# Decoder layer on one core: decay exponents from broadcast running sums instead of TensorE

## What is computed

```python
xBCzA = einsum('bld,od->blo', u, W_in)           # u: layernorm of x
xBC   = causal_depthwise_conv(xBC, conv_w, conv_b)  # 4 taps
dt    = softplus(A_log)
cum   = cumsum(-dt, axis=2)                       # within chunks of 128 tokens
CB    = einsum('bcqhn,bckhn->bchqk', C, B)
diff  = cumT[..., :, None] - cumT[..., None, :]
decay = exp(where(tril, diff, -inf))
y_intra = einsum('bchqk,bckhp->bcqhp', CB * decay, xdt)
# and across chunks: state from B * exp(cum_last - cum), y_inter from C * exp(cum)
out   = einsum('bli,oi->blo', (y_intra + y_inter + D * x) * silu(z + z_bias), W_out)
```

## Time and profile before

| what | before |
|---|---|
| median of 3 runs | 405.5 us (405.41 to 407.51) |
| the profiled execution's own time | 406.83 us |
| its span | 405.1 us |
| granted TensorE clock, mean | 0.996 |
| PE busy | 386.7 us (95%) |
| VectorE (DVE) busy | 332.6 us (82%) |
| ScalarE (ACT) busy | 226.6 us (56%) |
| GpSimd (POOL) busy | 176.2 us (43%) |
| chain that ended last | PE 70%, DVE 13%, ACT 8%, issue 6%, POOL 2% |
| DMA moved | 21.13 MB |

### The profile page before, as it was taken

The page is one execution under the profiler, slowest core; times in us unless marked ns, Lnnn a source line. Parts: engine busy times, 40 slices in busy tenths (PEclk is TensorE's granted clock), DMA queues, the critical chain, the costliest instruction groups (busy, mean ns, idle before and its releaser), DMA issues.

```text
span 405.1 us, 8904 instructions
## 1 busy us (share of the span) xinstructions
PE 386.7 (95%) x3023; PEld 299.3 (74%) x3023; DVE 332.6 (82%) x564; ACT 226.6 (56%) x422; POOL 176.2 (43%) x208
## 2 busy tenths in 40 slices
PE   8998999999999999996989999899999999999996
PEld 8686676766766767764767777568888888888886
DVE  5988899999999999997989938738958759696685
ACT  6766556465565564568676632664554545546541
...
GB/s 186 100 54 25 58 64 8 115 56 61 62 59 28 41 59 63 61 35 109 128 49 25 49 162 1 0 2 1 60 19 78 3 78 13 65 0 2 0 2 104
DMA packets 35932, 21.13 MB, mean 52 GB/s; under 512 B 17048, under 2 KB 33760, under 8 KB 35904
## 3 DMA queue, kind: packets, MB, share of 16 engines
...
...
## 4 chain that ended last, share of the span: by engine, by line
PE 70%; DVE 13%; ACT 8%; issue 6%; POOL 2%; ACTq 0%; DVEq 0%; POOLq 0%
PE bank L1283 22%; PE bank L1259 10%; PE bank L1249 9%; PE bank L1478 8%; PE bank L1252 5%; PE bank L1398 3%; PE bank L1269 2%; PE bank L1466 2%; DVE conv L1228 2%; PE bank L1307 2%; PE bank L1425 2%; DVE conv L1021 2%; POOL el L656 1%; ACT conv L695 1%; PE bank L1486 1%
## 5 line engine op out<-in xcount | busy, mean ns | idle before, releaser
L1021 DVE SCALAR_TENSOR_TENSOR conv<-bank,taps,conv 128x510 f32<-128x510 f32 (+2 forms) x204 | 149.8, 745 | 17.4 <-ACT conv L695 12.3
L1283 PE MATMUL bank<-uth,parts 128*128 128x512 f32 x272 | 95.3, 407 | 1.1 <-DVE utl L1004 0.9
L695 ACT ACTIVATE conv<-bank,tap_b,taps 128x512 f32<-128x512 f32 x68 | 52.9, 777 | 69.6 <-PE bank L1283 58.9
L569 POOL TENSOR_TENSOR ce<-conv,ecx 128x512 f32<-128x512 f32 x15 | 19.4, 1291 | 117.5 <-DVE conv L1021 117.5
L1283 PEld LDWEIGHTS bank<-uth,parts 128*128 128x128 f32 x272 | 51.0, 187 | 18.9 <-issue 3.5
L651 POOL TENSOR_TENSOR ul<-conv,uh 128x512 fp32r<-128x512 f32 x32 | 42.9, 1357 | 40.5 <-ACT uh L922 27.5
L656 POOL TENSOR_TENSOR el<-conv,parts 128x512 fp32r<-128x512 f32 x30 | 44.3, 1504 | 30.3 <-ACT parts L934 30.3
L1283 PE MATMUL bank<-utl,parts 128*128 128x512 f32 x136 | 53.5, 393 | 0.0
L1216 DVE CAST uh<-conv 128x512 fp32r<-128x512 f32 x28 | 26.0, 966 | 22.5 <-ACT conv L918 21.9
L1228 DVE TENSOR_TENSOR conv<-conv 128x512 f32<-128x512 f32 x32 | 31.4, 1014 | 11.9 <-ACT conv L939 11.8
L1106 DVE SCALAR_TENSOR_TENSOR g<-dec,bank 128x512 f32<-128x512 f32 x64 | 40.8, 678 | 0.0
(11 more groups left out here) (208 smaller groups left out, 743.3 us busy)
## 6 DMA issues: line engine op xcount, KB each, us to landing
w_raw<-in_L_attn_W_in_dram SPq DMA_DIRECT2D x17, 256.0 KB, 3.2
ecx<-ecum_dram SPq DMA_DIRECT2D x32, 128.0 KB, 2.9
ew_raw<-in_L_ffn_Wup_dram SPq DMA_DIRECT2D x7, 256.0 KB, 2.9
ew_raw<-in_L_ffn_Wgate_dram SPq DMA_DIRECT2D x7, 256.0 KB, 3.1
ew_raw<-in_L_ffn_Wdown_dram SPq DMA_DIRECT2D x7, 256.0 KB, 3.8
...
out_dram<-xres SPq DMA_DIRECT2D x4, 256.0 KB, 2.1
...
```

What stands on the lines that cost most here:

```text
L695: act.activation(conv[q][:, j, HALF * h:HALF * (h + 1)], bank[u % 2][:], ACT.Identity, bias=tap_b[q][:, j:j + 1], scale=taps[q][:, j, TAPS ...
L1021: dve.scalar_tensor_tensor(out=dst[:, :, d:SEQ], in0=src[:, :, 0:SEQ - d], scalar=taps[q][:, j, TAPS - 1 - d:TAPS - d], in1=dst[:, :, d:SE ...
L1283: ins = pe.matmul(bank[u % 2][:], w, x_t, start=(i == 0), stop=(i == 3 * KD - 1))
```

## The change

The running sums cum go to DRAM as float32 and come back broadcast over all 128 partitions, 256 KB for each unit of a pair (`load_cumb`, two DMAs for each half), into four buffers `cumb`, one for each unit. GpSimd masks each with an affine_select (`mask`). For half 0 it adds the column -cum_s (`spans`), and ScalarE takes one exponential over 512 columns (`decays`). For half 1 ScalarE adds the column as the bias of its exponential, which takes four instructions of 128 columns for each unit (`decays_beside`). The column comes from PE (two transposes of cum at the start), is negated by ScalarE into `ncum`, and is copied for each pair by GpSimd (`copy_ncum`). The exponent matmuls, their tables and the bf16 parts are gone. `turn_w` moves into the place of the first exponents.

DVE's taps are crossed: of two quarters v and v+1 the order is (v,1), (v,2), (v+1,1), (v,3), (v+1,2), (v+1,3), and those of quarter 3 move from the start of body n to the end of body n-1. The work for the later stages moves to earlier bodies: the gates of z to 8 and 9, the pairwise terms to 10 and 11, gate_y(0) to 11 and 12, the weight splits to 13 and 14.

```diff
-    cum_dram = nc.dram_tensor("cum_dram", (3, NH * T, P), BF16, kind="Internal").ap()
+    cum_dram = nc.dram_tensor("cum_dram", (NH * T, P), F32, kind="Internal").ap()
...
-            def load_cum(m, q):
-
-                at_least(sp, expo_done, 4 * (m - 2))
...
+            def load_cumb(m, h):
+
+                at_least(sp, exp_done, 4 * (m - 2) + 2 * h + 2)
+                for j in range(2):
+                    row = T * (2 * (m - 1) + j) + T // 2 * h
+                    sp.dma_start(cumb[2 * h + j][:],
+                                 cum_dram[row:row + T // 2, :].partition_broadcast(P)).then_inc(cumb_in[h], 16)
...
-                if n == 1:
-                    sp.wait_ge(cr0_done, 1)
-                if n < PAIRS:
-                    load_cum(n + 1, 1 - q)
+                if n > 1:
+                    load_cumb(n, 1)
...
                     load_w(n + 3, 1 - q)
                 if n + 2 <= PAIRS:
                     load_taps(n + 2, q)
+                if n < PAIRS:
+                    load_cumb(n + 1, 0)
...
+            def copy_ncum(m, q):
+
+                src = ncum[:].rearrange("p c (b h) -> p h b c", b=NSEQ)
+                pool.tensor_copy(ncp[q][:], src[:, bass.ds(2 * (m - 1), 2), :, :]).then_inc(ncp_done, 1)
+
+            def mask(u):
+
+                pool.affine_select(out=cumb[u][:], in_=cumb[u][:], compare_op=ALU.is_ge, fill=NEG, base=0,
+                                   pattern=[[0, T // 2], [1, P]], channel_multiplier=-1).then_inc(masked, 1)
+
+            def spans(n, q, u):
+
+                pool.wait_ge(masked, 4 * (n - 1) + u + 1)
+                from_s = ncp[q][:, u, 0:2, :].rearrange("p b c -> p (b c)").unsqueeze(2).to_broadcast([P, T // 2, P])
+                pool.tensor_tensor(cumb[u][:], cumb[u][:], from_s, ALU.add).then_inc(span_done, 1)
...
+                pool.wait_ge(cumb_in[0], 32 * n)
+                pool.wait_ge(ncp_done, n)
                 if end:
+                    pool.wait_ge(cumb_in[1], 32 * n)
+                    for u in range(4):
+                        mask(u)
+                    spans(n, q, 0)
+                    spans(n, q, 1)
                     decay_c_half(n, q, 0)
                     decay_c_half(n, q, 1)
...
+                    gate_late()
+                    rest_weights(1, 1, 1)
+                    rest_weights(1, 1, 2)
+                    return
+                at_least(pool, stT_done, n - 1)
+                copy_xs(n + 1, 1 - q)
+                mask(0)
+                mask(1)
+                spans(n, q, 0)
+                spans(n, q, 1)
+                at_least(pool, y_done, 4 * (n - 1))
+                copy_x(n + 1, 1 - q)
+                decay_c(n, k, q)
+                pool.wait_ge(cumb_in[1], 32 * n)
+                at_least(pool, exp_done, 4 * (n - 1))
+                copy_ncum(n + 1, 1 - q)
+                mask(2)
+                mask(3)
+                if not isinstance(n, int):
+                    return
+                if n == 1:
+                    weigh_context()
+                if n in (PAIRS - 7, PAIRS - 6):
+
+                    for v in range(2 * (n - PAIRS + 7), 2 * (n - PAIRS + 7) + 2):
                         pool.wait_ge(zgate_done, v + 1)
                         pool.tensor_tensor(z_part(v), z_part(v), zgate(v), ALU.mult).then_inc(z_gated, 1)
...
+                if n in (PAIRS - 5, PAIRS - 4):
+                    pool.wait_ge(z_gated, 4)
+                    gate_y(0, n - PAIRS + 5)
+                if n == PAIRS - 3:
+                    pool.wait_ge(sig_done, T)
+                    pool.tensor_scalar(sig[:], sig[:], P_SEM / 2, P_SEM / 2, ALU.mult, ALU.add).then_inc(sig_scaled, 1)
+                    rest_weights(0, 0, 0)
+                if n == PAIRS - 2:
+                    rest_weights(0, 0, 1)
+                    rest_weights(0, 0, 2)
+                    rest_weights(1, 1, 0)
+                if n == PAIRS - 1:
+                    gate_y(1, 0)
+                    gate_y(1, 1)
...
             def decays(n, u):
-                a, b = 4 * (n - 1) + u, u % 2
-                act.wait_ge(expo_done, a + 1)
-                at_least(act, g_done, a - 1)
-                act.activation(dec[b][:], bank[4 + b][:], ACT.Exp).then_inc(exp_done, 1)
+                a = 4 * (n - 1) + u
+                act.wait_ge(span_done, 2 * (n - 1) + u + 1)
+                at_least(act, g_done, a - 3)
+                act.activation(dec[u][:], cumb[u][:].rearrange("p i t -> p (i t)"), ACT.Exp).then_inc(exp_done, 1)
+
+            def decays_beside(n, q, u, chunks):
+
+                if chunks[0] == 0:
+                    act.wait_ge(masked, 4 * (n - 1) + u + 1)
+                    act.wait_ge(ncp_done, n)
+                    at_least(act, g_done, 4 * (n - 2) + u + 1)
+                for i in chunks:
+                    ins = act.activation(dec[u][:, i * P:(i + 1) * P], cumb[u][:, i, :], ACT.Exp,
+                                         bias=ncp[q][:, u % 2, 2 + i // 2, i % 2:i % 2 + 1])
+                if chunks[-1] == T // 2 - 1:
+                    ins.then_inc(exp_done, 1)
...
+                decays_beside(n, q, 2, range(4))
                 if first:
                     act.wait_ge(y_init, 1)
                 else:
                     act.wait_ge(cb_done, 2 * (n - 1))
-                    act.wait_ge(ce_done, n - 1)
                 beside(n, m, km, r, 0)
+                decays_beside(n, q, 3, range(2))
                 beside(n, m, km, r, 1)
                 copy_b(n)
-                decays(n, 2)
-                decays(n, 3)
+                decays_beside(n, q, 3, range(2, 4))
                 copy_state_turned(n)
+                if not first:
+                    act.wait_ge(ce_done, n - 1)
                 beside(n, m, km, r, 2)
                 beside(n, m, km, r, 3)
...
+            def crossed_taps(m, q, v):
+
+                done = 12 * m + 3 * v
+                for i, (u, d) in enumerate(((v, 1), (v, 2), (v + 1, 1), (v, 3), (v + 1, 2), (v + 1, 3))):
+                    j, h = u // 2, u % 2
+                    src = bank[u % 2][:].rearrange("p (b l) -> p b l", b=2)
+                    dst = conv[q][:, j, HALF * h:HALF * (h + 1)].rearrange("p (b l) -> p b l", b=2)
+                    if d == 1:
+                        dve.wait_ge(acc_first, 4 * m + u + 1)
+                    else:
+                        dve.wait_ge(tap_done, done + (0, 1, 0, 2, 3, 5)[i])
+                    dve.scalar_tensor_tensor(
+                        out=dst[:, :, d:SEQ], in0=src[:, :, 0:SEQ - d], scalar=taps[q][:, j, TAPS - 1 - d:TAPS - d],
+                        in1=dst[:, :, d:SEQ], op0=ALU.mult, op1=ALU.add).then_inc(tap_done, 1)
...
-                        other_taps(n + 1, 1 - q, 0)
-                        other_taps(n + 1, 1 - q, 1)
+                        crossed_taps(n + 1, 1 - q, 0)
                     dve.wait_ge(exp_done, a + 1)
                     dve.wait_ge(cb_done, 2 * (n - 1) + u // 2 + 1)
                     at_least(dve, y_done, a - 1)
 
-                    dve.scalar_tensor_tensor(out=g[b][:], in0=dec[b][:], scalar=1.0, in1=bank[2 + b][:],
+                    dve.scalar_tensor_tensor(out=g[b][:], in0=dec[u][:], scalar=1.0, in1=bank[2 + b][:],
                                              op0=ALU.min, op1=ALU.mult).then_inc(g_done, 1)
                     if u == 3 and not last(n, 1):
-                        other_taps(n + 1, 1 - q, 2)
+                        crossed_taps(n + 1, 1 - q, 2)
...
-            pe.transpose(bank[7][:, 0:P], sdecT[:], ident[:]).then_inc(sdec_turned, 1)
+            pe.transpose(bank[7][:, 0:P], sdecT[:], ident[:])
+            for c in range(2):
+                ins = pe.transpose(bank[7][:, (1 + c) * P:(2 + c) * P], cum[:, c * P:(c + 1) * P], ident[:])
+            ins.then_inc(sdec_turned, 1)
...
-            def exponents(n, k, q, u):
-
...
-                for a in range(2):
-                    ins = pe.matmul(bank[4 + j][NS * a:NS * (a + 1), :], cl[q][:, j, NS * a:NS * (a + 1)],
-                                    cr[q][a][:, j, 4 * h:4 * h + 4, :].rearrange("p t k -> p (t k)"), start=True, stop=True)
-                ins.then_inc(expo_done, 1)
...
-                    exponents(n, k, q, 0)
-                    exponents(n, k, q, 1)
+                    turn_w(n + 2, k + 1, q, lambda: None)
                 else:
                     end_pair(n, k, q)
-                if not last(n, 2):
-                    turn_w(n + 2, k + 1, q, lambda: None)
                 b_dot_c(n, q, 0)
                 passes(m, r, 0, range(6))
                 passes(m, r, 1, range(6))
                 turn_b(n, q)
-                exponents(n, k, q, 2)
-                exponents(n, k, q, 3)
...
                 weigh(n - 1, 1 - q, 2)
-                exponents(n, k, q, 0)
-                exponents(n, k, q, 1)
+                if not last(n, 2):
+                    turn_w(n + 2, k + 1, q, lambda: None)
                 from_state(n - 1, 0)
```

186 lines of the change are left out of this document (57 added, 129 removed).

## The result

Slower: **461.1 us** (median of 4 runs, 457.2 to 462.2) against 405.8 before on the same chip, a ratio of 1.134 with a 95% interval of 1.126 to 1.141. The sign and the mechanism are as forecast; the 442 us are 19 us short, and the time is 2 us outside the range of 428 to 459. The profiled execution has a span of 459.0 us.

The account below looks back on a forecast made before the run. A loop through the SP queue was to set each pair at 14.8 us; start +3.2, pairs +22.3 and +0.5, tail +13.9, end -3.2 summed to +36.7 us, a median of 442.2, range 428 to 459.

Parts of the forecast that it names:

- The loop that is closed: Pair stage: half-0 loads queue behind the write of y, so each pair's y hangs on the last: 14.8 us per pair.
- Two loads: lands 3.2 us after its issue: In the pair's loop: the second half-0 load starts 0.65 us after the first and lands 3.2 us after issue.
- My own upper end, 3.8: Half-0 loads in the pair's loop: a landing of 3.8 us would make the loop 15.4 us.
- SP from Y(n-1) ... 6.04: In the pair's loop: SP's queue takes 6.04 us from ScalarE's copy of y to where the next half-0 load can start.
- GpSimd and ScalarE, 4.9: End of the pair's loop: GpSimd's copy, masks and additions 4.0 us, then ScalarE's second decay 0.5 and y copy 0.37.
- the line through 0.30 and 0.40: GpSimd's masks: affine_select times for 128 and 256 columns, extended to 0.60 us for 512.
- The clock: Rival: PE stands still for 3.5 of 14.8 us per pair, so its clock falls: 458 us, chance 0.08.
- The broadcast lands late: Rival in the pair's loop: dear masks or a landing of 4.6 us add 1.4 per pair: 462 us, chance 0.06.
- Tail: From ScalarE's copy of pair 13's y to pair 15's: 38.2 us against 24.3 today, +13.9.
- Start: Up to ScalarE's copy of pair 1's y: decay 1 ends later than today, +3.2 us.
- After Y(15): Behind ScalarE's copy of pair 15's y: PE has C·B, turn_b and the first output tile done, no exponents: -3.2 us.
- The queue does not bind: 397: Rival in the pair stage: SP's queue does not bind and pairs fall to DVE's 11.6 us: some 397, chance 0.05.

Follow-up runs that it names:

- the fillers: Eight extra 512-column matmuls per pair, from 1 to 15, placed where TensorE waits, added to the changed kernel: 454.8 us.
- the run with the four pieces: On top of the fillers, the write of the 1024 sums cut into four and the experts' loads put a pair later, behind half 0: 462.5 us.
- contiguous sums: On top of the fillers, the 1024 sums written to DRAM as 128 pieces of 32 bytes in place of 1024 of 4 bytes: 453.8 us.
- the queue open: Changed kernel with SyncE's part reordered, next pair's half-0 broadcast first and its half-1 broadcast last, late z and y loads spread over six parts: 433.9 us.

## Why the prediction was right, and where it failed

- **The loop that is closed**: right. Two more issues in the loop and moving the half-0 load both changed the pair as it says, and the plain pair at 14.78 us is the 14.8 forecast.
- **"Two loads: lands 3.2 us after its issue"**: this is the step that failed most, +11.0 us. The forecast has 0.65 + 3.2 = 3.85 from the first issue to GpSimd's start. It was 4.2 to 4.7 in plain pairs and 5.0 to 5.9 in the last four, 4.77 on average. The second issue came 0.47 behind the first. The first load landed 3.5 us after its issue in the median of the twelve pairs, near w_raw's 3.3, but the second, for which GpSimd waits as well, 4.2 on average (3.5 to 5.4). I had costed the second of two broadcasts as a lone load of weights. My own upper end, 3.8, was nearer. The three loads of experts' weights that stand behind half 0 at Y(9) and Y(10) are a part of it: issue to start is 5.5 and 5.2 there in after, 5.15 and 5.3 with the fillers. In the run with the four pieces they stood behind half 0 at Y(10) and Y(11) instead, and Y(9) fell to 4.6, Y(10) stayed at 5.2 and Y(11) rose from 4.1 to 5.1. In after the ones at Y(11) and Y(12) were 5.0 and 5.9 without such loads, and 4.1 and 4.6 with the fillers, for no reason that a run isolates. Nor did any run load a half without broadcast, so what a broadcast costs more than a plain load is not shown. The 2.6 us estimated from the Trainium skill (DMA: Bandwidth & Descriptors, section Anatomy of one DMA), which I had put aside, would have been further off.
- **"SP from Y(n-1) ... 6.04"**: right in the pairs without anything odd and 1.0 to 2.0 longer in four, +5.6 in all. One, +2.0 at Y(2), stands behind the write of the sums and was gone with contiguous sums. All four stand in pairs in which the instruction queue moved 16 KB during the issues (at 72.0 in the one at Y(2)); that was not tested, and how much of each it makes stays open.
- **GpSimd and ScalarE, 4.9**: 4.5 to 4.6 but for the pair at Y(7), as one addition takes 1.04 us and not the 1.29 of the product of C (1042 ns is the mean of one in the page's costliest groups). The masks were 0.61 to 0.64, as taken from the line through 0.30 and 0.40.

```profile
L498 POOL TENSOR_TENSOR cumb<-cumb,ncp 128x512 f32<-128x512 f32 x32 | 32.7, 1042 | 0.0
```

- **The clock** was a rival at 0.08 with 16 us. It took part, with 6.3 us, beside the main case; I had treated them as alternatives. Of the 6.3, 4.8 lie between Y(1) and Y(13), so they are inside the 14.2: the pair at Y(7), where TensorE was late, had 2.7 us more than the others behind GpSimd's start and 1.1 with the fillers. The lateness came from the gates of z, which the prediction priced at 0.5 in all. With the fillers the landing term is still 9.2 us above the forecast, so the clock does not explain it.
- **"The broadcast lands late", a rival at 0.06 with 462**: its time is the one that was measured, but in part by luck. The landing was 0.9 us per pair longer and not 1.4, the masks were not dear, and the rest came from issues and the clock.
- **Tail**: 39.5 against 38.2. **Start**: +4.2 against +3.2. **After Y(15)**: -2.5 against -3.2. All near.
- **"The queue does not bind: 397"**: with the queue open the change gives 434, not 397. The ring over ce and the masks of half 1 was not in the prediction. I had added up ScalarE's path to the state copy, 10 us, but not asked what GpSimd waits for before those masks. It did not bind here, so it cost the forecast nothing, but it would have made that rival wrong.

The odd pairs were not all removed by any run: fillers and contiguous sums together gave 453.8, not the 442 forecast. In that run issue to GpSimd's start was 53.8 us over the twelve pairs against the 46.2 of the forecast, so most of what is left is the landing, which no run changed by itself.
